# Context rows of the second cross attention in two halves, late moments and context norms between the first one's tiles

## The reference, cut to what matters

```
x = x + tanh(g_xattn[0]) * _L0_xattn_ref(_layernorm(x), ctx, ctx, ...)        # X0
x = x + tanh(g_ffn[0])   * _L0_ffn_ref(_layernorm(x), router, experts ...)    # F0: best of 8 experts
x = x + tanh(g_xattn[1]) * _L1_xattn_ref(_layernorm(x), ctx, ctx, mask, ...)  # X1
...
# in X1, with ctx of 77 rows a batch:
q = layer_norm(query @ Wq, gq, bq)
k = layer_norm(ctx @ Wk, gk, bk)
v = layer_norm(ctx @ Wv, gv, bv)
```

## Time and profile before

| what | before |
|---|---|
| median of 3 runs | 1052.25 us |
| lowest and highest | 1049.93 and 1054.67 us |
| the profiled execution, first to last instruction | 1057.6 us |
| PE, DVE busy over it | 87%, 74% |
| ACT, POOL busy over it | 53%, 46% |
| loop of X0, first scores to last update | 17.1 to 111.6 us |
| gate of F0 | 119.6 to 122.5 us |

### The profile page before, as it was taken

One profiled execution on the slowest core, in us unless ns is written; L12 is line 12 of the kernel. 1 busy time (PEld: TensorE's weight loads), 2 busy tenths in 40 slices (PEclk: granted clock), 3 DMA queues, 4 the chain that ended last, 5 costly groups with the idle time before them and its releaser, 6 DMA issues.

```text
span 1057.6 us, 19542 instructions
## 1 busy us (share of the span) xinstructions
PE 919.4 (87%) x6337; PEld 655.6 (62%) x6337; DVE 785.7 (74%) x2080; ACT 557.7 (53%) x1494; POOL 490.0 (46%) x451
## 2 busy tenths in 40 slices
PE   6898985888778999869997598988989999989987
PEld 4787533767578989727775243434437677768774
DVE  6889999999756777769998376777734744589982
ACT  4675456886444445724443156766764233445533
POOL 5444553555066564635556777574530600024430
PEclk9999896999879999969999659989999999999998
DMA  9300000000111111410000322222102000000001
GB/s 324 149 1 1 2 6 1 1 1 1 41 39 39 41 40 33 109 66 1 0 1 0 107 67 62 82 76 62 31 1 101 1 1 1 1 2 2 1 1 40
DMA packets 29828, 40.55 MB, mean 38 GB/s; under 512 B 11468, under 2 KB 25036, under 8 KB 29228
## 3 DMA queue, kind: packets, MB, share of 16 engines
q1 hardware_dynamic: 27244, 34.28, 10.3%
q0 software_dynamic: 2496, 5.16, 1.9%
HBM read 31.44 MB, written 7.82 MB: 37 GB/s over the span
## 4 chain that ended last, share of the span: by engine, by line
PE 27%; issue 14%; POOL 7%; DVE 5%; ACT 3%; SPq 1%; DMA 0%; DVEq 0%; POOLq 0%; ACTq 0%
POOL att L1787 6%; PE ps L1163 4%; PE ps L829 4%; PE ps L1135 4%; PE ps L819 4%; PE ps L1147 3%; PE ps L793 1%; PE ps L1249 1%; PE ps L1257 1%; DVE rs L2124 1%; PE ps L1101 1%; DVE stats L2001 0%; SPq L570 0%; PE ps L1106 0%; DVE U L2029 0%
## 5 line engine op out<-in xcount | busy, mean ns | idle before, releaser
L1787 POOL TENSOR_TENSOR att<-att,ri 128x1232 f32<-128x1232 f32 x64 | 169.3, 2645 | 190.5 <-DVE ri L2130 190.5
L793 PE MATMUL ps<-VW,PT 128*128 128x128 f32 (+3 forms) x1280 | 157.6, 278 | 17.5 <-DVE x L2145 16.0
L793 PEld LDWEIGHTS ps<-VW,PT 128*128 128x128 f32 (+1 forms) x1280 | 148.4, 192 | 35.2 <-DVE x L2145 28.3
L1369 ACT ACTIVATE PT<-ps 128x512 f32<-128x512 f32 x128 | 70.6, 594 | 89.5 <-PE ps L766 88.7
L766 PE MATMUL ps<-W,att 128*128 128x128 f32 (+1 forms) x640 | 86.9, 282 | 16.2 <-POOL att L1787 14.7
L1761 POOL TENSOR_TENSOR rstd<-ve,minus_half 128x4 f32<-128x4 f32 x38 | 38.8, 1039 | 114.2 <-DVE ve L2016 97.7
L900 PE MATMUL ps<-PT,att 128*128 128x128 f32 x624 | 80.8, 285 | 8.5 <-issue 8.4
L829 PEld LDWEIGHTS ps<-U,att 128*128 128x128 f32 x512 | 66.3, 191 | 33.1 <-issue 29.1
L766 PEld LDWEIGHTS ps<-W,att 128*128 128x128 f32 (+1 forms) x640 | 72.7, 143 | 22.3 <-POOL att L1787 15.5
L2581 DVE CUSTOM_DVE_ANT_0 C<-ps,cmaskb 128x512 bf16<-128x512 f32 (+1 forms) x128 | 71.1, 555 | 20.7 <-PE ps L1135 18.0
L2581 DVE CUSTOM_DVE_ANT_0 U<-ps,cmaskb 128x384 bf16<-128x384 f32 (+1 forms) x128 | 53.9, 421 | 41.8 <-PE ps L1135 41.5
(11 more groups left out here) (432 smaller groups left out, 2105.6 us busy)
## 6 DMA issues: line engine op xcount, KB each, us to landing
U<-in_ffn SPq DMA_DIRECT2D x1, 6176.0 KB, 23.2
U<-split SPq DMA_DIRECT2D x144, 32.0 KB
W<-split SPq DMA_DIRECT2D x144, 32.0 KB
W<-in_packed SPq DMA_DIRECT2D x1, 2162.5 KB, 23.5
U<-in_ffn SPq DMA_DIRECT2D x1, 2060.0 KB, 9.7
U<-in_moe SPq DMA_DIRECT2D x1, 2048.0 KB, 7.3
split<-VBD SPq DMA_DIRECT2D x4, 384.0 KB, 2.9
split<-W SPq DMA_DIRECT2D x4, 384.0 KB, 2.7
```

The costliest lines, as they stand in the source:

```text
L793: q = mm(attended(s, t), PT[0:m, t.slot(2), c, :], batch(VW, t.group)[0:m, c * D:(c + 1) * D], start=(c == 0), stop=(c == NC - 1))
L1369: go(PT[:, t.slot(2), 4 * k:4 * k + 4, :].rearrange("p c n -> p (c n)"), ps[:, k0 + k, :], ACT.Copy).then_inc(probsT, 1)
L1787: tt(p, p, over_keys(ri[:, t.slot(2), :]), ALU.mult).then_inc(probs, 1)
```

## The change

- PE makes the context rows of X1 in two calls: batches 0 and 1 where all four stood, batches 2 and 3 and the means behind the query projection of batch 0, ahead of the first scores. The second half takes banks 5 and 4, so the first folding of values waits for ACT's copies of them. ACT's copies are split in the same way.
- DVE makes only batch 1's moments ahead of the loop of X0. A new last action of each of its first six steps, `first_rows`, makes batch 2's moments (step 0), batch 3's (step 1), the moments of the context's keys and values (steps 2 and 3), the sum with `1wq` and the normalized key rows (step 4), and the normalized value rows (step 5). The last two wait for a new action of POOL, `context_root`, behind its third `normalize`. What they replace in F0 is gone.
- POOL makes batch 1's offsets behind batch 1's root. Batches 2 and 3's roots and offsets move behind the second spreading of values. Its two roots of the context in F0 become the one of `context_root`.
- DVE and POOL have the loop of X0 written out, 16 tiles in a row. Some semaphores are merged.

The core of the diff:

```
-                    for b in range(B):
-                        mm(ps[0:KEYS, 2 + b // 2, (b % 2) * 2 * D:(b % 2 + 1) * 2 * D],
-                           w("ctxT")[:, b * KEYS:(b + 1) * KEYS], w("1wkv"), start=True, stop=True)
-                    pe.wait_ge(consts, 1)
-                    mm(ps[:, 0, 0:D], minus_half[:, 0:1].to_broadcast([P, P]), w("1wq"), start=True, stop=True).then_inc(kv_ps, 1)
+                    for b in (2 * part, 2 * part + 1):
+                        t = mm(ps[0:KEYS, RAW_BANK[part], (b % 2) * 2 * D:(b % 2 + 1) * 2 * D],
+                               w("ctxT")[:, b * KEYS:(b + 1) * KEYS], w("1wkv"), start=True, stop=True)
+                    if part == 1:
+                        pe.wait_ge(consts, 1)
+                        t = mm(ps[:, 4, 0:D], minus_half[:, 0:1].to_broadcast([P, P]), w("1wq"), start=True, stop=True)
+                    t.then_inc(kv_ps, 1)
...
             mm(ps[:, 6, :], w("0wq"), xnT_s[:, :], start=True, stop=True).then_inc(q_ps, 1)
+            keys_values(X1, 1)
             first_cross()
...
# POOL
                 if b == 0:
                     root(ROUND0[X0] + 1, 1)
+                    set_offset(0, slice(TB, 2 * TB), ROUND0[X0] + 2)
+                elif b == 1:
                     root(ROUND0[X0] + 2, 2)
                     root(ROUND0[X0] + 3, 3)
-                    set_offset(0, slice(TB, NT), ROUND0[X0] + B)
+                    set_offset(1, slice(2 * TB, NT), ROUND0[X0] + B)
...
+                def context_root(t):
+                    if t.n == 2:
+                        pool.wait_ge(context_chain, KV1 * (2 * TB + 1))
+                        tt(c_rstd[0:KEYS, :], c_ve[0:KEYS, :], minus_half[0:KEYS, 0:1].to_broadcast([KEYS, KV1 * TB]), ALU.pow)\
+                            .then_inc(consts, 1)
...
# DVE
+                def first_rows(t):
+                    if s != X0:
+                        return
+                    if t.n + 2 < B:
+                        dve.wait_ge(rows_in[t.n + 2], 16)
+                        moments(ROUND0[X0] + t.n + 2, rows_of(x, t.n + 2), t.n + 2)
+                    elif t.n < 2 + KV1:
+                        context_moments(t.n - 2)
+                    elif t.n < 2 + 2 * KV1:
+                        dve.wait_ge(consts, 2)
+                        if t.n == 2 + KV1:
+                            tt(w("1wq"), means_s, w("1wq"), ALU.add).then_inc(consts, 1)
+                        context_normed(t.n - 2 - KV1)
...
-            for b in range(1, B):
-                dve.wait_ge(rows_in[b], 16)
-                moments(ROUND0[X0] + b, rows_of(x, b), b)
+            dve.wait_ge(rows_in[1], 16)
+            moments(ROUND0[X0] + 1, rows_of(x, 1), 1)
...
-            for r in range(KV1):
-                moments(n0 - KV1 + r, kv[r], r, rows=KEYS)
-            tt(w("1wq"), means_s, w("1wq"), ALU.add).then_inc(consts, 1)
...
-            normed_context(0)
             gate(F0, 0, 0, tg[:, 4:5])
-            normed_context(1)
```

More of the change, by code:

```diff
@@ L64, in before @@
     return sum(B * table[i] for i in range(s)) + (kv if s > X1 else 0)
-ROUND0 = {s: before(ROUNDS, s, KV1) + (KV1 if s == X1 else 0) for s in range(9)}
+ROUND0 = {s: before(ROUNDS, s, 0) for s in range(9)}
 TURN0 = {s: before(TURNED, s, 1) + (1 if s == X1 else 0) + (B - 1 if s == X0 else 0) for s in range(9)}
@@ L94 @@
 RINGS = 3
+OUT_CHAIN = (E - HALF - 1) * NT
+ROPE_CHAIN = OUT_CHAIN + UNITS
+SELECT_CHAIN = ROPE_CHAIN + 2 * B
 HOLD = 4
@@ L666, in fold_values @@
                 pe.wait_ge(vbd, n + 1)
+                if s == X0 and b == 0:
+                    pe.wait_ge(kv_sb, KV_SB0[X3])
                 pe.wait_ge(vw_sb, n + (3 if s == X0 else 1))
@@ L1315, in keys_values @@
                         go(v_to, ps[:, k0 + 1, 0:CK], ACT.Identity, bias=b_[:, 2:3]).then_inc(kv_sb, 1)
[L1316 to L1320, removed]
+                elif s == X1:
+                    act.wait_ge(kv_ps, KV_PS0[X1] + part + 1)
+                    t = go(raw_rows[:, part * 4 * D:(part + 1) * 4 * D], ps[0:KEYS, RAW_BANK[part], :], ACT.Copy)
+                    if part == 1:
+                        go(means_s, ps[:, 4, 0:D], ACT.Copy, scale=2.0 / D).then_inc(kv_sb, 1)
                 else:
@@ L1787, in normalize @@
                     tt(p, p, over_keys(ri[:, t.slot(2), :]), ALU.mult).then_inc(probs, 1)
-                skewed_loop(pool, [(normalize, 0)], NT, TB)
+                def context_root(t):
[3 more added lines that the diff above has]
+                            .then_inc(consts, 1)
+                if s == X0:
+                    skewed_loop(pool, [(normalize, 0), (context_root, 0)], NT, NT)
+                else:
+                    skewed_loop(pool, [(normalize, 0)], NT, TB)
             pool.wait_ge(ld["a"], 16)
@@ L2030, in normed, with raw_row, context_moments, context_normed @@
                             .then_inc(s_xn, rounds)
+            def raw_row(r, i):
+                return raw_rows[:, (KV1 * i + r) * D:(KV1 * i + r + 1) * D]
+            def context_moments(r):
+                at = slice(r * TB, (r + 1) * TB)
+                made = (2 * TB + 1) * r
+                dve.wait_ge(kv_sb, KV_SB0[X3])
+                for i in range(TB):
+                    v.bn_stats(c_stats[0:KEYS, r * TB + i, :], raw_row(r, i)).then_inc(context_chain, 1)
+                dve.wait_ge(context_chain, made + TB)
+                for i in range(TB):
+                    v.bn_aggr(c_mv[0:KEYS, r * TB + i, :], c_stats[0:KEYS, r * TB + i, :]).then_inc(context_chain, 1)
+                dve.wait_ge(context_chain, made + 2 * TB)
+                ts(c_ve[0:KEYS, at], c_mv[0:KEYS, at, 1], LN_EPS, None, ALU.add).then_inc(context_chain, 1)
+            def context_normed(r):
+                for i in range(TB):
+                    k = r * TB + i
+                    ts(kv_rows[r][:, i, :], raw_row(r, i), c_mv[0:KEYS, k, 0:1], c_rstd[0:KEYS, k:k + 1],
+                       ALU.subtract, ALU.mult).then_inc(context_xn, 1)
             def xn_of(nth):
@@ L2157, in cross @@
                     steps = [(largest, 0), (shift, 0), (total, 1), (invert, 1)]
-                skewed_loop(dve, steps + [(last_rope, 0), (update, 3), (early_moments, 3)], NT, TB)
+                skewed_loop(dve, steps + [(last_rope, 0), (update, 3), (early_moments, 3), (first_rows, 0)], NT, NT if s == X0 else TB)
             def gate(s, n, base, tanh):
```

52 lines of the change are left out of this document (27 added, 25 removed).

## The result

The changed kernel takes 1066.53 us (median of four runs, 1064.9 to 1067.62), the kernel before beside it 1052.66. The ratio is 1.0136, with a 95% interval of 1.0108 to 1.0164: slower by 11 to 17 us.

The account below looks back on a forecast made before the run. The program was taken as one chain of stages, X0's loop as a circle over DVE and PE. 9.05 + 7.25 - 0.4 = 15.9 us on the median of 1052.25 gave 1068.2 us, range 1062 to 1072.

Parts of the forecast that it names:

- likeliest case: Whole kernel: the forecast of 1068.2 us itself, given chance 0.61 and its own range of 1066 to 1070.5.
- the fill: From first matmul to X0's fourth maximum, until the loop runs with all its engines: 9.05 us longer.
- the norms: X0's steps 3 to 5: context rows behind the update are held until POOL's `normalize` ends, costing 7.25 us.
- F0: Stage after X0's loop: 1.5 us won behind the gate, 1.1 lost ahead of it, net -0.4 us.
- The wait of POOL: Start of X0: POOL waits for batch 2's and 3's late moments, so the first `normalize` begins 9.05 us later.
- taken back: Rival, start of X0: the fill has slack, so the late first `normalize` costs nothing; 1057.7 us, chance 0.05.
- The halves: PE's start: context rows of X1 in two halves bring the first scores 1.4 us earlier.
- The bound of 2.3: PE's start: upper end for earlier first scores, 2.3 us if the moved half is wholly covered.
- not held: Rival, X0's steps 3 to 5: context rows slip past `normalize`, costing 2.25 us; 1063.2 us, chance 0.20.
- The rival's price for the unheld work: X0's steps 3 to 5: context rows of 1.47, 1.39 and 1.11 us less DVE's idle time cost 2.25 us.
- The loop written out: X0's loop: DVE's and POOL's branch and register rows go, nothing waits for them, so 0.
- The clock rival: PE's clock also falls behind its longer waits, in two more stretches of 1.7 us; 1071.6 us, chance 0.11.

Follow-up runs that it names:

- Experiments one: Changed kernel with batch 2's and 3's moments put back ahead of DVE's first maximum: 1057.49 us, ratio 1.006 to the kernel before.
- two: Changed kernel with POOL's roots and offsets of batches 2 and 3 moved behind the first `normalize`, DVE's moments left: 1059.75 us, ratio 1.0079.
- kernel three: Changed kernel with DVE's four context actions moved from behind the update to between shift and sum: 1064.75 us, ratio 1.0137.
- five: Kernel before with only PE's and ACT's part of the change, the context rows in two halves: 1052.16 us, ratio 1.0005.
- four: Changed kernel with POOL's gain and bias of X1's value rows moved from F0 behind `normalize` 12 and 13 in X0's loop: 1066.97 us, ratio 1.0146.

## Why the prediction was right, point by point

**Sum and sign.** 1068.2 was forecast, 1066.53 measured, inside the likeliest case's own range. The forecast sum of 15.9 us has 15.8 in the trace, but by misses that cancel: the fill 0.65 more, the norms 1.59 less, F0 0.99 more.

**The wait of POOL: right in mechanism and size.** The two idle times, the first `normalize` at 36.97 (36.6 forecast), the fourth maximum at 43.08 (42.7) and PE's one wait of 11.65 us all came. Experiments one and two show the cause from both sides: the fill's 9.70 us go when the moments go back, and 6.98 of them when only the wait goes. The other 2.7 are the moments between the tiles, which the forecast had on the same path. The rival "taken back" falls: at the end of X1 nothing of the fill's delay had come back.

**The halves: the step that failed.** 1.4 us earlier scores were forecast, and 0.2 came. The term assumed that the products behind the shorter block keep the length they had; at the lower level the projection and the second half together lost about 1.8 us (2.08 - 1.12 and 1.91 - 1.03). The bound of 2.3 fits the other case, 2.1 in kernel three. That the level rises later behind a shorter block is not shown, as said under five; that it was the lower one here is. The fill is longer for it by 1.2 us; that it ends only 0.65 above the forecast is due to the rest, from first maximum to first `normalize`, which took 19.42 us instead of the 36.6 - 16.6 = 20.0 forecast.

**Context norms: mechanism right, size too large.** 7.25 forecast, 5.66 measured. By steps (from maximum to maximum, 3 to 7), before 5.34, 5.45, 5.24, 5.54, 5.19; after 6.81, 7.79, 7.63, 4.63, 5.56. Steps 3 to 5 cost 6.20, forecast 7.25; step 6 gives 0.91 back, for its scores were ready and its maximum waited for nothing; the forecast had excluded that anything is given back. And in step 4 the addition was added to the hold, where it ran beside `normalize` for its 0.28 and took that off the time that the next row was held. The rival "not held" falls by the rows themselves, and experiment three prices the holding at 2.81 of the 5.66. The rival's price for the unheld work, 2.25, fits: 2.85 there, less the wait of 0.62.

The Trainium skill ("SBUF — State Buffer", section "Who interferes with whom") says that a `tensor_tensor` with both inputs in SBUF contends with GpSimd's reads too. The addition at 54.52, 0.02 us behind `normalize`, took 0.28 all the same, and `normalize` 2.40 instead of 2.25: the addition lost nothing here, and `normalize` 0.15 us. The key spreading before, a `tensor_tensor` too, did lengthen beside POOL's gain and bias: 3.12 us for three rows against 1.64 for four. So one short addition does not speak against what the Trainium skill says. With its rule in the same section for `tensor_scalar` the trace agrees, in shapes that before did not show, 77x128 and 77x4.

**F0: signs right, one size off.** To the gate 1.1 was set as lost and 2.31 came: the holding, 4.40 against 2.36, and products at the lower level behind it. Behind the gate 1.5 was set as won; from the gate to the second batch of experts 8.83 us became 7.50, 1.33 less, with 2.56 for four rows of key spreading instead of 3.51. DVE before and after:

```profile
124.96 3.51 DVE L2071 TENSOR_TENSOR KBD<-att,W 128x308 f32<-128x308 f32 x4
...
128.39 1.50 DVE L2476 SCALAR_TENSOR_TENSOR x<-ps,w_all,x 128x128 f32<-128x128 f32 x4
```

```profile
141.84 2.56 DVE L2120 TENSOR_TENSOR KBD<-att,W 128x308 f32<-128x308 f32 x4 [0.18 <-ACT att L1562]
144.33 1.50 DVE L2528 SCALAR_TENSOR_TENSOR x<-ps,w_all,x 128x128 f32<-128x128 f32 x4
```

From there to X1's first offset it is 35.37 us instead of 35.76. Net +0.59 instead of -0.4.

**The loop written out** was set at 0. No run isolates it; from the ninth maximum to the last update, where the change has nothing else, 50.89 us became 50.73.

**The clock rival** came in part: granted 0.50 from 33 us to about 44. Up to 39.27 that is PE's own wait, with nothing to slow. Behind it PE worked at the lower level, as it had before behind its shorter wait, and it cost no more: from the end of the first `normalize` to the fourth maximum it is 3.86 us, before 3.82. In steps 5 to 7 the clock did not fall, as the mean of 0.99 shows (PE behind its wait, then the stretch from fourth to ninth maximum with its columns as in the earlier trace rows, the clock third from the end):

```profile
39.27 2.40 PE L779 MATMUL ps<-W,att 128*128 128x128 f32 x10 [11.65 <-POOL att L1803]
...
43.08:75.50 32.42, 27.03 (x223) 22.55 (x224) 31.15 (x44) 18.27 (x46) 11.77 (x6) 0.99 0.00 1
```

It did not cost the 3.4 us. Kernels two and four had such a fall, from 64.0 to 67.4 us and from 62.8 to 66.3; in two it cost some 1.6 us, and in four nothing shows of it (32.41 us for steps 3 to 7).

## What to carry to other kernels

Work moved "between" tiles is only free if nothing that stands early in another engine's fixed order waits for it: follow the moved result to the instruction that waits for it, and then to everything queued behind that one. On DVE, put `tensor_scalar` rows where no POOL elementwise instruction runs; right behind an instruction that releases POOL is a bad place, and a row of four elements a partition cost about a microsecond there. A start that is made earlier pays only as far as the next engine's queue is ready for it, and its rows must be costed at both levels of PE's clock.

## What the runs showed of the hardware that was not expected

The page's clock column reads 1.00 for PE from 6 to 18 us in after and in kernel five, while rows there last nearly twice as long as the same rows later (1.99 for four products, 1.03 later; projection 2.07 against 1.12). At the start the rows' lengths tell the level and the column does not. In each of the eleven traces the first record of the granted clock begins where the rows become short, at 12.7 us before, 16.7 after and 18.2 in kernel five; the column counts the time ahead of it, which has no record, as full.

A POOL power of 77x8 took 1.66 us, one of 128x4 1.01: with fewer partitions and more elements in each it took longer.
